# Seven block products for eight: a three-network MLP on one TensorE, with its weight operands kept in memory

## The chip, the cores and the metric

One core of a Trainium2 chip runs the whole program. The metric is the device time of one execution in microseconds (us), the median of three runs. Engines are named as in the profile: PE (matrix multiply), PEld (its weight load), DVE (vector), ACT (scalar), POOL (GpSimd) and SP (the queue that issues the DMAs).

## The reference, cut to what matters

The input x is 2 sequences of 2048 tokens with 512 features, in float32. Three two-layer networks (two shared, one chosen per sequence) with 2048 inner units run on every token. They are mixed with three gate weights per sequence, which depend on its first token, and a 512x512 layer chosen per sequence follows.

```
def _dense(x, wi_, wo_):
    return jax.nn.relu(x @ wi_) @ wo_
...
s0 = _dense(x, swi[0], swo[0]);  s1 = _dense(x, swi[1], swo[1])
h = jax.nn.relu(jnp.einsum('bsd,bdf->bsf', x, wi_sel))
eo = jnp.einsum('bsf,bfd->bsd', h, wo_sel)
gate_in = jnp.concatenate([eo[:, 0], s0[:, 0], s1[:, 0]], axis=-1)
w = jax.nn.softmax(jax.nn.relu(gate_in @ g1) @ g2, axis=-1)
x = x + eo * w[:, 0] + s0 * w[:, 1] + s1 * w[:, 2]
x = x + (x @ W[cat] + b[cat])
```

## The kernel before, in words

Precision comes from splitting. Each float32 operand becomes a high part, rounded to fp32r by ACT, and a low part, the rest, by DVE. `product` then does three matmuls for each one of the mathematics (high by high, low by high, high by low), 128x128 weights against 512 tokens each.

The 4096 tokens are taken in four *supers* of 1024, two blocks of 512. A super goes through 24 slices of 256 inner units, 8 for each network. For a slice SP loads the raw weights (`load_weights`), ACT makes the high parts (`split_high`) and DVE the low ones (`split_low`), so every super splits every weight again. PE runs *units*: `up` gives 128 inner units of one block in PSUM (`hps`), ACT and DVE turn them into `hh` and `hl` with the relu, `down` multiplies them into four PSUM banks (`yps`), and DVE adds these to `Y` in SBUF (`accumulate`). While PE runs one unit's `down`, the next unit's `up` is already done: the order is written out by hand in `steps`, and engines meet by semaphores only. Each engine takes its instructions in order, SP too.

Between supers the tokens of the next are transposed by PE (`transpose_x`). The sums are mixed by DVE (`mix`) in the first units of the next super, and the category layer (`category`, 48 full-width matmuls a block) runs after units 5 and 7 there, with `out_tiles` taking its result from PSUM. The gate of a sequence is computed once, at the end of its first super (`gate_partial`, `gate_hidden`, `gate_logits`). POOL clears buffers and rebuilds tokens (`xaux`, `gaux`) as high plus low.

Of the kernel before, what the change touches and what calls it, by code (L numbers as in the profile page):

```python
# [12 lines left out]
P = 128  # L31
D = 512
F = 2048
# [7 lines left out]
GC = GF // P  # L41
GROUPS = NETS * F // GF
PAIRS = GROUPS // 2
NET_PAIRS = PAIRS // NETS
WCOLS = KD * GF + GC * D
PIECE = 512
PIECES = WCOLS // PIECE
WARM_UP = 6
UNITS = 8
GATE_PART = [1, 2, 0]  # L50

def mixed(s):

    return NETS * KD * s

def mix_net(s):

    return 0 if s == SUPERS - 1 else 2  # L60

def build(nc, x, expert_id, category_id, wi, wo, swi, swo, g1, g2, W, bias, out):

# [9 lines left out]

    ctx = ExitStack()
    with ctx:
        def sb(name, shape, dt=F32):
            return ctx.enter_context(nc.sbuf_tensor(name, shape, dt))

        def sem(name):  # L80
            return ctx.enter_context(nc.semaphore(name))

        xh = sb("xh", [P, 2, 2, KD, TB], F32R)
        xl = sb("xl", [P, 2, 2, KD, TB], F32R)

        Y = sb("Y", [P, NETS, 2, KD, TB])
        wh = sb("wh", [P, 2, WCOLS], F32R)
        wl = sb("wl", [P, 2, WCOLS], F32R)  # L90
        wraw = sb("wraw", [P, 2, WCOLS])
        hh = sb("hh", [P, 2, TB], F32R)
        hl = sb("hl", [P, 2, TB], F32R)
        Wh = sb("Wh", [P, KD, D], F32R)
        Wl = sb("Wl", [P, KD, D], F32R)
        xaux = sb("xaux", [P, KD, TB])
        gaux = sb("gaux", [P, KD, D])
        gacc = sb("gacc", [P, D])
        bias_bc = sb("bias_bc", [P, D])
        ident = sb("ident", [P, P])  # L100
        ones = sb("ones", [P, P])
        g2s = sb("g2s", [P, KD, NETS])
        gt = sb("gt", [P, KD])
# [6 lines left out]
        ids = sb("ids", [1, 4], I32)  # L110

        yps = [ctx.enter_context(nc.psum_tensor(f"yps{j}", [P, TB], F32)) for j in range(KD)]
        hps = [ctx.enter_context(nc.psum_tensor(f"hps{j}", [P, TB], F32)) for j in range(2)]

        aps = [ctx.enter_context(nc.psum_tensor(f"aps{j}", [P, TB], F32)) for j in range(2)]

        s_ids = sem("ids_loaded")
        s_x = [sem("x_loaded_even"), sem("x_loaded_odd")]
        s_x0 = [sem("first_tokens_loaded_0"), sem("first_tokens_loaded_1")]
        s_w0 = [sem("first_up_weights_loaded_0"), sem("first_up_weights_loaded_1")]  # L120
        s_w0rdy = sem("first_up_weights_ready")
        s_w = [sem("weights_loaded_0"), sem("weights_loaded_1")]
        s_g = sem("gaux_loaded")
        s_g2 = sem("g2_loaded")
        s_bias = sem("bias_loaded")
        s_stored = [sem("out_stored_block_0"), sem("out_stored_block_1")]
        s_c = sem("ident_set")
        s_ident = sem("ident_cleared")
        s_ones = sem("ones_set")
        s_xtr = sem("x_transposed")  # L130
        s_xhi = sem("x_high_split")
        s_xlo = sem("x_low_split")
        s_whi = sem("weights_high_split")
        s_wrdy = sem("weights_ready")
        s_hps = sem("hidden_in_psum")
        s_hhi = sem("hidden_high_split")
        s_hrdy = sem("hidden_ready")
        s_yps = sem("net_out_in_psum")
        s_yacc = sem("net_out_accumulated")
        s_zero = sem("net_out_cleared")  # L140
        s_gused = sem("gaux_used")
        s_gch = sem("gate_vector_step")
        s_gps = sem("gate_product_in_psum")
        s_grelu = sem("gate_hidden_ready")
        s_gexp = sem("gate_exp_ready")
        s_gmix = sem("gate_product_ready")
        s_gmax = sem("gate_max_ready")
        s_xs = sem("x_summed")
        s_mix = [sem("mix_step_block_0"), sem("mix_step_block_1")]
        s_chi = sem("x2_high_split")  # L150
        s_clo = sem("x2_low_split")
        s_Wi = sem("category_identity_added")
        s_Whi = sem("category_high_split")
        s_Wrdy = sem("category_ready")
        s_ops = sem("out_in_psum")
        s_oev = sem("out_evacuated")

        block = ctx.enter_context(nc.Block())

        @block.sync
        def _(sp):
            def load_weights(s, net, p, j, e):

                m = s * GROUPS + net * 2 * NET_PAIRS + 2 * p + j
                f0 = p * 2 * GF + j * GF
                c0 = p * 2 * GC + j * GC
                if not isinstance(m, int) or m >= 2:
                    sp.wait_ge(s_wrdy, m - 1)
                src_i, src_o, n = (swi_v, swo_v, net) if net < 2 else (wi_v, wo_v, e)  # L170
                sp.dma_start(wraw[:, j, 0:KD * GF].rearrange("p (k f) -> p k f", k=KD),
                             src_i[n, :, :, bass.ds(f0, GF)]).then_inc(s_w[j], 16)
                sp.dma_start(wraw[:, j, KD * GF:WCOLS].rearrange("p (c d) -> p c d", c=GC),
                             src_o[n, :, bass.ds(c0, GC), :]).then_inc(s_w[j], 16)

            for h in range(2):
                ks = slice(2 * h, 2 * h + 2)
                sp.dma_start(xaux[:, :, 2 * h * P:(2 * h + 2) * P],  # L180
                             x_blk[0, :, :, 2 * h * P:(2 * h + 2) * P]).then_inc(s_x0[h], 16)
# [570 lines left out]
```

## Time and profile before

| | |
|---|---|
| median of 3 runs | 2220.74 us (2220.53 to 2221.44) |
| span of the profiled execution | 2218.0 us |
| PE busy | 2204.1 us (99%), 9772 instructions |
| DVE, ACT, POOL busy | 50%, 21%, 3% |
| DMA | 126.93 MB, mean 57 GB/s |
| PE clock | nine tenths or more of full speed in all 40 slices |

The table is to be read with care at one place: busy time of PE counts the modelled end of overlapping matmuls, so a matmul's mean duration is not its share of the time. Starts are what counts for PE. For DVE, ACT and POOL durations are real, and neighbours overlap by a little.

### The profile page before, as it was taken

How to read it: one execution, taken by the hardware profiler on the slowest of the kernel's cores; microseconds unless marked ns; L12 is line 12 of the kernel's file. 1: busy time of each engine (PE TensorE's matmuls, PEld its weight loads, DVE VectorE, ACT ScalarE, POOL GpSimd, SP SyncE). 2: the span in 40 equal slices, each digit the busy share in tenths (PEclk: the TensorE clock that was granted, in tenths of full speed). 3: DMA queues.
4: the chain of work that ended last, by engine and by line, in shares of the span. 5: the costliest groups of instructions: out<-in, count | busy, mean ns of one | idle time of the engine just before them, and what ended most of it. 6: DMA issues, size and time to landing. Idle time of an engine off the chain costs nothing.

```text
span 2218.0 us, 26621 instructions
## 1 busy us (share of the span) xinstructions
PE 2204.1 (99%) x9772; PEld 1825.4 (82%) x9772; DVE 1115.2 (50%) x1784; ACT 471.3 (21%) x847; POOL 65.8 (3%) x29
## 2 busy tenths in 40 slices
PE   9999999999999999999999999999999999999999
PEld 7888888887888888888888888888878888888887
DVE  4445454446744444444564455454466444444456
ACT  3212121222221212122212212121221221212121
POOL 1000000001000000000100000000010100000000
PEclk9999999999999999999999999999999999999999
DMA  3112121111111211111212121211111211111100
GB/s 133 62 57 87 46 76 57 57 38 57 57 57 57 67 46 57 38 57 38 76 38 100 38 95 38 76 62 51 57 57 38 76 38 57 38 57 43 52 19 39
DMA packets 85569, 126.93 MB, mean 57 GB/s; under 512 B 4116, under 2 KB 54292, under 8 KB 83732
## 3 DMA queue, kind: packets, MB, share of 16 engines
q1 hardware_dynamic: 85524, 126.37, 16.7%
q8 instruction: 23, 0.38, 0.1%
q14 instruction: 22, 0.18, 0.0%
HBM read 117.97 MB, written 8.39 MB: 57 GB/s over the span
## 4 chain that ended last, share of the span: by engine, by line
PE 99%; issue 0%; DMA 0%; DVE 0%; SPq 0%; ACT 0%; DVEq 0%
PE hps L602 47%; PE yps L602 47%; PE aps L602 4%; PE aps L642 1%; DMA xaux<-in_x_dram 0%; DVE gp L434 0%; PE aps L659 0%; ACT hh L295 0%; DVE hl L374 0%; DVE Y L491 0%; SPq L180 0%; SPq L182 0%; DVEq L395 0%
## 5 line engine op out<-in xcount | busy, mean ns | idle before, releaser
L374 DVE SCALAR_TENSOR_TENSOR hl<-hps,hh 128x512 fp32r<-128x512 f32 x384 | 265.1, 690 | 1033.9 <-ACT hh L295 1031.8
L602 PE MATMUL hps<-xh,wh 128*128 128x512 f32 x1536 | 600.4, 391 | 0.0
L602 PE MATMUL hps<-xh,wl 128*128 128x512 f32 x1536 | 599.2, 390 | 0.0
L602 PE MATMUL hps<-xl,wh 128*128 128x512 f32 x1536 | 599.1, 390 | 0.0
L602 PE MATMUL yps<-hh,wh 128*128 128x512 f32 x1536 | 598.3, 390 | 0.0
L602 PE MATMUL yps<-hh,wl 128*128 128x512 f32 x1536 | 597.7, 389 | 0.0
L602 PE MATMUL yps<-hl,wh 128*128 128x512 f32 x1536 | 597.5, 389 | 0.0
L295 ACT ACTIVATE hh<-hps 128x512 fp32r<-128x512 f32 x384 | 229.6, 598 | 1676.9 <-PE hps L602 1676.9
L396 DVE TENSOR_TENSOR Y<-yps,Y 128x512 f32<-128x512 f32 x728 | 450.0, 680 | 0.0
L602 PEld LDWEIGHTS hps<-xh,wl 128*128 128x128 f32 x1536 | 289.2, 188 | 60.3
L602 PEld LDWEIGHTS hps<-xh,wh 128*128 128x128 f32 x1536 | 289.1, 188 | 60.0 <-DVE wl L557 0.4
L602 PEld LDWEIGHTS hps<-xl,wh 128*128 128x128 f32 x1536 | 289.3, 188 | 59.7
L602 PEld LDWEIGHTS yps<-hh,wh 128*128 128x128 f32 x1536 | 288.6, 188 | 59.9
L602 PEld LDWEIGHTS yps<-hh,wl 128*128 128x128 f32 x1536 | 288.2, 188 | 60.1
L602 PEld LDWEIGHTS yps<-hl,wh 128*128 128x128 f32 x1536 | 288.5, 188 | 59.7
L382 DVE TENSOR_TENSOR wl<-wraw,wh 128x512 fp32r<-128x512 f32 x382 | 238.4, 685 | 0.0
L302 ACT ACTIVATE wh<-wraw 128x512 fp32r<-128x512 f32 x382 | 208.6, 623 | 0.0
L280 POOL TENSOR_TENSOR xaux<-xh,xl 128x2048 f32<-128x2048 f32 x4 | 18.4, 4612 | 1448.0 <-issue 919.7
L602 PE MATMUL aps<-Wl,xh 128*128 128x512 f32 x128 | 49.8, 389 | 0.0
L602 PE MATMUL aps<-Wh,xh 128*128 128x512 f32 x128 | 49.8, 389 | 0.0
L602 PE MATMUL aps<-Wh,xl 128*128 128x512 f32 x128 | 49.8, 389 | 0.0
L491 DVE TENSOR_TENSOR Y<-aps,bias_bc 128x512 f32<-128x512 f32 x32 | 22.0, 689 | 47.8 <-PE aps L602 47.8
(52 smaller groups left out, 382.5 us busy)
## 6 DMA issues: line engine op xcount, KB each, us to landing
wraw<-in_L_cond_swi_dram SPq DMA_DIRECT2D x63, 512.0 KB, 3.4
wraw<-in_L_cond_swo_dram SPq DMA_DIRECT2D x63, 512.0 KB, 4.7
wraw<-in_L_cond_wi_dram SPq DMA_DIRECT2D x32, 512.0 KB, 3.4
wraw<-in_L_cond_wo_dram SPq DMA_DIRECT2D x32, 512.0 KB, 4.8
out_dram<-Y SPq DMA_DIRECT2D x7, 1024.0 KB, 4.0
gaux<-in_L_cond_g_dram SPq DMA_DIRECT2D x6, 1024.0 KB, 8.1
xaux<-in_x_dram SPq DMA_DIRECT2D x6, 1024.0 KB, 6.0
gaux<-in_L_cond_W_dram SPq DMA_DIRECT2D x2, 1024.0 KB, 7.9
```

The costliest lines, as they stand in the source:

```text
L280: pool.tensor_tensor(into[:, :, :], xh[:, q, k, :, :].bitcast(F32), xl[:, q, k, :, :].bitcast(F32), ALU.add).then_inc(s_xs, 1)
L295: act.activation(hh[:, i % 2, :], hps[i % 2][:, :], ACT.Relu).then_inc(s_hhi, 1)
L302: act.activation(wh[:, slot, cols], wraw[:, slot, cols], ACT.Copy).then_inc(s_whi, 1)
L374: dve.scalar_tensor_tensor(out=hl[:, i % 2, :], in0=hps[i % 2][:, :], scalar=0.0, in1=hh[:, i % 2, :].bitcast(F32), op0=ALU.max, op1=ALU.s ...
L382: last = dve.tensor_tensor(wl[:, slot, cols], wraw[:, slot, cols], wh[:, slot, cols].bitcast(F32), ALU.subtract)
L396: dve.tensor_tensor(Y[:, net, k, d, :], yps[d][:, :], Y[:, net, k, d, :], ALU.add).then_inc(s_yacc, 1)
L491: dve.tensor_tensor(Y[:, 1, k, t, :], aps[T % 2][:, :], bias_bc[:, :], ALU.add).then_inc(s_oev, 1)
L602: last = pe.matmul(dst, stationary[a], moving[b], start=start and i == 0, stop=stop and i == 2)
L642: last = pe.transpose(aps[X % 2][:, t * P:(t + 1) * P], src[:, t, d * P:(d + 1) * P], ident[:, :])
```

## The change

The product of a token matrix and a weight matrix is cut into 2x2 blocks: tokens by block of 512 (two) and features by half (two), weights likewise. Seven products of sums of blocks replace the eight (Strassen's scheme in Winograd's form). One *step* is now a slice of 256 inner units of one network for all 1024 tokens; there are 96. In a step PE runs seven `up` products and seven `down` products, each of six full-width matmuls, alternating: `up(n, i)` of the next step, then `down(d, i)` of this one. I call the time of one such alternation a *period*.

What the seven products need in addition:

- Sums of token blocks (`XT`), once a super, by POOL (`token_sum`).
- Sums of weight blocks, by POOL (`up_sums`, `down_sums`, four subtractions or additions each). They are split and, in the 24 steps of super 0 and the 8 of the other sequence's own network (super 2, network 2), written by SP to memory (`keep_up`, `keep_down`). These 32 steps are called *prepared*. In the other 64 the split sums are read back, product by product (`load_up`, `load_down`), and nothing is split.
- Sums of hidden blocks: DVE combines the seven up results (`block_step`, five a step), ACT applies the relu, POOL subtracts (`hidden_sums`), ACT and DVE split.
- Seven accumulators `ACC` of 1024 elements. DVE adds each product's pair of PSUM banks (`add_sum`), ACT copies in a network's first step of an even super (`begin_sum`). Where a network ends the sums go to memory (`spill`) and come back as `MB` or `MR` for mixing in the next super, a quarter at a time, with `mix_scale` (DVE) and `mix_add` (POOL).

Down products, tokens' transposes, gate and category results all go through a ring of two PSUM pairs `rps`: `next_pair` waits until the entry two before was taken. The category layer now has 12 parts of 24 matmuls in supers 1 to 3, each behind `up(n, 4)`, and four at the end.

```
-                for d in range(KD):
-                    if c == 0 and not (isinstance(K, int) and K == 0):
-                        pe.wait_ge(s_yacc, KD * K + d + 1 - KD)
-                    c0 = KD * GF + c * D + d * P
-                    last = product(yps[d][:, :], (wh[:, slot, c0:c0 + P], wl[:, slot, c0:c0 + P]),
-                                   (hh[:, v % 2, :], hl[:, v % 2, :]), c == 0, c == GC - 1)
+            def next_pair(kind, i):
+                e = turn[0]
...
+                turn[0] += 1
+                if e >= 2:
+                    pe.wait_ge(*taken(e - 2))
+                return rps[e % 2]
+            def up(n, i):
...
+                for q in range(2):
+                    cols = slice(q * P, (q + 1) * P)
+                    toks = slice(q * TB, (q + 1) * TB)
+                    ins = product(ups[UP_BANK[i]][:, :], (WU[:, i, 0, cols], WU[:, i, 1, cols]),
+                                  (XH[:, i, toks], XL[:, i, toks]), q == 0 and i < 4, q == 1)
+            def down(n, i):
+                dst = next_pair("sum", PRODUCTS * n + i)
...
+                for j in range(2):
+                    cols = slice(j * P, (j + 1) * P)
+                    ins = product(dst[:, j, :], (WD[:, i, 0, cols], WD[:, i, 1, cols]),
+                                  (HH[:, i, :], HL[:, i, :]), True, True)
+            def category(s, c):
+                dst = next_pair("out", 4 * s + c)
+                pe.wait_ge(s_ml, 4 * s + c + 1)
...
+            for m in range(-1, STEPS):
+                n, d = m + 1, m
+                for i in range(PRODUCTS):
+                    if n < STEPS:
+                        up(n, i)
+                    for kind, k in ring_extra(m, i):
...
+                    if d >= 0:
+                        down(d, i)
```
The sums by POOL, and the way of the raw down blocks: SP may load new ones only when the low parts of the last are made.
```
+            def hidden_sums(n):
...
+                pool.tensor_tensor(HT[:, 2:4, :], hid[:, 1:3, :], hid[:, 0:2, :], ALU.subtract).then_inc(s_T, 1)
...
+                pool.tensor_tensor(HT[:, 4, :], hid[:, 2, :], HT[:, 2, :], ALU.subtract).then_inc(s_T, 1)
...
+                pool.tensor_tensor(HT[:, 6, :], HT[:, 5, :], HT[:, 4, :], ALU.subtract).then_inc(s_T, 1)
+            def blocks_down(n, experts):
+                if PREP[n] >= 1:
+                    sp.wait_ge(s_wld, 2 * PREP[n])
...
+                for slot, a, c in ((0, 0, 0), (7, 1, 0), (6, 1, 1), (5, 0, 1)):
+                    sp.dma_start(PD[:, slot, :], src[e, :, c0 + c, a * HB:(a + 1) * HB]).then_inc(s_pd, 16)
+            def down_high(n, late):
...
+                act.wait_ge(s_Sd, 4 * PREP[n] + (4 if late else 3))
+                act.activation(WD[:, part, 0, :], PD[:, part, :], ACT.Copy).then_inc(s_whd, 1)
+            def down_low(n, late):
...
+                dve.tensor_tensor(WD[:, part, 1, :], PD[:, part, :], WD[:, part, 0, :].bitcast(F32),
+                                  ALU.subtract).then_inc(s_wld, 1)
```

Two places show how the queues stand. The first is DVE in a weight-splitting stretch. Before, it has four splits of 512 (`wl`) between two hidden low parts (`hl`), and four adds (L396) after every second of these, here in the first slices:
```order
L374 SCALAR_TENSOR_TENSOR hl<-hps,hh 128x512
L382 TENSOR_TENSOR wl<-wraw,wh 128x512 x4
L374 SCALAR_TENSOR_TENSOR hl<-hps,hh 128x512
L396 TENSOR_TENSOR Y<-yps,Y 128x512 x4
L374 SCALAR_TENSOR_TENSOR hl<-hps,hh 128x512 x2
```
Now, in a whole prepared period, it has these (`WU`, `WD` are low parts of weights, `HL` of hidden blocks, `ACC` the adds, the three rows at L951 `block_step`):
```order
L887 TENSOR_TENSOR WU<-PU,WU 128x4x256
L903 TENSOR_TENSOR HL<-HT,HH 128x1024
L923 TENSOR_TENSOR ACC<-rps,ACC 128x1024
L893 TENSOR_TENSOR WD<-PD,WD 128x4x256
L906 TENSOR_TENSOR HL<-HT,HH 128x1536
L923 TENSOR_TENSOR ACC<-rps,ACC 128x1024 x2
L887 TENSOR_TENSOR WU<-PU,WU 128x3x256
L951 TENSOR_TENSOR u_59<-ups,p_58 128x512
L951 TENSOR_TENSOR u_60<-ups,u_59 128x512
L951 TENSOR_TENSOR hid<-ups,u_60 128x512
L923 TENSOR_TENSOR ACC<-rps,ACC 128x1024
L893 TENSOR_TENSOR WD<-PD,WD 128x3x256
```
Behind these come an add, the low part of `hid`, and two block steps with an add behind each. Splits now stand between the adds on which PE's ring waits, and read buffers that POOL has written.

The second place is a period with a part of the category layer, on DVE. Its result leaves PSUM at L1030 now:
```order
L926 SCALAR_TENSOR_TENSOR ACC<-rps,gw,ACC 128x1024 [waits sum_added,down_product]
L1022 TENSOR_TENSOR MXL<-MX,MXH 128x1024 [waits mix_high]
L926 SCALAR_TENSOR_TENSOR ACC<-rps,gw,ACC 128x1024 [waits sum_added,down_product]
L899 TENSOR_TENSOR HL<-hid,HH 128x1024 [waits hidden_high_parts]
L951 TENSOR_TENSOR hid<-ups,u_59 128x512 [waits up_product]
L1030 TENSOR_TENSOR OUT<-rps,bias_bc 128x1024 [waits bias_loaded,out_in_psum]
```
On PE, in the same period, the 24 category matmuls (their last is the first row here) stand ahead of `down(d, 4)`:
```order
L1179 MATMUL rps<-WcH,MXL 128x512
L1179 MATMUL rps<-HH,WD 128x512 [waits down_operand_loaded_4,hidden_low_parts,sum_added]
L1179 MATMUL rps<-HL,WD 128x512
L1179 MATMUL rps<-HH,WD 128x512 x2
L1179 MATMUL rps<-HL,WD 128x512
L1179 MATMUL rps<-HH,WD 128x512
L1179 MATMUL ups<-XH,WU 128x512 [waits up_operand_loaded_5,hidden_block_step]
L1179 MATMUL ups<-XL,WU 128x512
L1179 MATMUL ups<-XH,WU 128x512 x2
L1179 MATMUL ups<-XL,WU 128x512
L1179 MATMUL ups<-XH,WU 128x512
L1179 MATMUL rps<-HH,WD 128x512 [waits down_operand_loaded_5,hidden_low_parts,out_evacuated]
```
Before, these matmuls had two PSUM buffers (`aps`) of their own; now they hold a pair of the ring of the down products, and `down(d, 5)` waits for its release.

## Rows read from the trace of the kernel before

**Rows 1.** The page: busy time, granted clock, the chain that ended last
```profile
PE 2204.1 (99%) x9772; PEld 1825.4 (82%) x9772; DVE 1115.2 (50%) x1784; ACT 471.3 (21%) x847; POOL 65.8 (3%) x29
PEclk9999999999999999999999999999999999999999
PE 99%; issue 0%; DMA 0%; DVE 0%; SPq 0%; ACT 0%; DVEq 0%
```
**Rows 2.** Timeline (start, duration), PE: first and last of 96 category matmuls
```profile
2192.36 0.39 PE L602 MATMUL aps<-Wh,xh 128*128 128x512 f32 x1
...
2213.90 0.39 PE L602 MATMUL aps<-Wh,xl 128*128 128x512 f32 x1
```
**Rows 3.** Timeline, start of the program: first up matmul, eight transposes, first down
```profile
10.41 0.77 PE L602 MATMUL hps<-xh,wh 128*128 128x512 f32 x1
...
17.90 1.04 PE L642 MATMUL aps<-ident,gaux 128*128 128x128 f32 x8
...
18.69 0.47 PE L602 MATMUL yps<-hh,wh 128*128 128x512 f32 x1
```
**Rows 4.** Timeline, PE around the first gate; idle time before in brackets
```profile
546.25 1.05 PE L659 MATMUL aps<-gp,ones 128*128 128x3 f32 x8 [3.16 <-DVE gp L434]
...
548.30 0.63 PE L602 MATMUL hps<-xl,wh 128*128 128x512 f32 x1
548.73 0.63 PE L602 MATMUL hps<-xh,wl 128*128 128x512 f32 x1
...
551.29 0.47 PE L602 MATMUL hps<-xh,wl 128*128 128x512 f32 x1
```
**Rows 5.** Timeline, end of the program, DVE's last instruction
```profile
2214.32 0.69 DVE L491 TENSOR_TENSOR Y<-aps,bias_bc 128x512 f32<-128x512 f32 x1 [2.03 <-PE aps L602]
```
**Rows 6.** Timeline, DVE and ACT: four instructions back to back
```profile
546.11 2.47 DVE L396 TENSOR_TENSOR Y<-yps,Y 128x512 f32<-128x512 f32 x4
553.03 2.49 DVE L382 TENSOR_TENSOR wl<-wraw,wh 128x512 fp32r<-128x512 f32 x4
19.55 2.20 ACT L302 ACTIVATE wh<-wraw 128x512 fp32r<-128x512 f32 x4
```
**Rows 7.** The page's costliest groups: ACT, busy us, mean ns, idle before
```profile
L295 ACT ACTIVATE hh<-hps 128x512 fp32r<-128x512 f32 x384 | 229.6, 598 | 1676.9 <-PE hps L602 1676.9
```
**Rows 8.** Timeline, POOL: memsets of 4096 and 2048, additions of 2048
```profile
5.00 3.51 POOL L269 MEMSET Y<- 128x4096 f32 x1
...
541.38 4.54 POOL L280 TENSOR_TENSOR gaux<-xh,xl 128x2048 f32<-128x2048 f32 x1
...
1732.44 1.81 POOL L288 MEMSET Y<- 128x2048 f32 x1 [27.56 <-DMA out_dram<-Y]
...
1738.78 4.62 POOL L280 TENSOR_TENSOR gaux<-xh,xl 128x2048 f32<-128x2048 f32 x1
```
**Rows 9.** Timeline, DVE while POOL adds
```profile
536.89 1.29 DVE L403 TENSOR_TENSOR xl<-aps,xh 128x512 fp32r<-128x512 f32 x2 [1.15 <-ACT xh L308]
540.70 5.50 DVE L434 TENSOR_SCALAR gp<-g2s,gt 128x3 f32<-128x3 f32 x4
1742.28 3.47 DVE L382 TENSOR_TENSOR wl<-wraw,wh 128x512 fp32r<-128x512 f32 x4
```
**Rows 10.** DMA: issue of one on SP; by line, KB and median us to landing; queue's bytes and share
```profile
305.87 0.37 SPq L171 DMA_DIRECT2D wraw<-in_L_cond_wi_dram  x1
...
wraw<-in_L_cond_swi_dram SPq DMA_DIRECT2D x63, 512.0 KB, 3.4
out_dram<-Y SPq DMA_DIRECT2D x7, 1024.0 KB, 4.0
gaux<-in_L_cond_g_dram SPq DMA_DIRECT2D x6, 1024.0 KB, 8.1
out_dram<-Y SPq DMA_DIRECT2D x4, 256.0 KB, 2.5
q1 hardware_dynamic: 85524, 126.37, 16.7%
```

More of the change, by code:

```diff
@@ new lines, in net_of, with slice_of, prepared, weight_set @@
+def net_of(n):
+    return n % STEPS_SUPER // STEPS_NET
+def slice_of(n):
+    return n % STEPS_NET
+def prepared(n):
+    return n < STEPS and (super_of(n) == 0 or (super_of(n) == 2 and net_of(n) == 2))
+def weight_set(n):
+    return net_of(n) * STEPS_NET + slice_of(n) + (STEPS_NET if net_of(n) == 2 and super_of(n) >= 2 else 0)
+PREP = [sum(prepared(i) for i in range(n)) for n in range(STEPS + 1)]
+SETS = (NETS + 1) * STEPS_NET
+def copied(n):
+    return slice_of(n) == 0 and (super_of(n) % 2 == 0 or net_of(n) == 0)
@@ new lines, in build, with taken @@
+        s_tail = sem("tail_pool_step")
+        s_tadd = sem("tail_vector_step")
+        plan = ring_plan()
+        place_in_ring = {entry: e for e, entry in enumerate(plan)}
+        def taken(e):
+            kind, i = plan[e]
+            if kind == "tokens":
+                return s_xs, i + 1
+            if kind == "gate":
+                b = sum(1 for o in plan[:e] if o == (kind, i))
+                return (s_grelu, b + 1) if i == 0 else (s_gexp, b + 1)
+            if kind == "out":
+                return s_oev, i + 1
+            n = i // PRODUCTS
+            if copied(n):
+                return s_acp, PRODUCTS * COPIES[n] + i % PRODUCTS + 1
+            return s_acc, i + 1 - PRODUCTS * COPIES[n]
@@ L349, in _, with staged @@
[L349 to L367 removed]
+            def staged(k, h):
+                return XS[:, k, h, :, :].rearrange("p j t -> p (j t)")
@@ L728, in _ @@
-            for k in range(2):
-                category(SUPERS - 1, k)
+                pe.matmul(ups[3][:, 0:P], ones[:, :], ones[:, :], start=True, stop=True)
+            for i in range(4):
+                transpose_tokens(i)
+            for m in range(-1, STEPS):
+                n, d = m + 1, m
+                for i in range(PRODUCTS):
+                    if n < STEPS:
+                        up(n, i)
+                    for kind, k in ring_extra(m, i):
+                        if kind == "tokens":
+                            transpose_tokens(k)
+                        elif kind == "out":
+                            category(k // 4, k % 4)
+                        elif k == 0:
+                            gate_hidden(m // (2 * STEPS_SUPER))
+                        else:
+                            gate_logits(m // (2 * STEPS_SUPER))
+                    if d >= 0:
+                        down(d, i)
```

1502 lines of the change are left out of this document (969 added, 533 removed).

## The prediction

> **What bounds the kernel now.** I read the page first, for the busiest engine and the last chain: PE is busy 99% of the span and the chain that ended last lies on it for 99% [rows 1]. The reader is to see that nothing else is near: DVE 50%, POOL 3%. So the time is PE's matmuls, and I need their spacing, not their duration. The timeline gives it: 96 category matmuls start from 2192.36 to 2213.90, 95 gaps, so 0.2267 us each [rows 2]. A full-width product of six takes U = 1.36 us. 9600 matmuls (9216 of the networks, 384 of the category layer) make 2176 of 2218 us. Then I looked at the ends [rows 3, 5], at the one place where PE stands, the gate [rows 4], and at what DVE, ACT, POOL and the DMAs cost apiece [rows 6 to 10], since the change loads these.
>
> **What it removes.** Each step has 7 x 12 = 84 matmuls for 96: 96 x 84 + 384 = 8448, 1152 fewer. At 0.2267 that is -261.2 us. The profiled execution would go from 2218.0 to 1956.8. A period of 14 products is 19.05 us if PE never waits. All else below is added.
>
> **DVE's price list.** Four adds of 512 take 2.47 us and one 0.69 [rows 6, 5]: 0.60 apiece back to back, of which 0.53 is 512 elements and 0.06 fixed. So 1024 costs 1.13, 1536 1.66, 768 0.86. The low parts of weights go alike (2.49 for four). A plain period has seven adds (7.9), five block steps (3.0, and 0.3 as three wait for one another) and low parts of 1024, 1024, 1536 (3.9): 15.1 us under 19.05. ACT does four of 512 in 2.20 and one in 0.60 [rows 6, 7], so I take 1.04 for 1024; it has about 6 us. POOL: memsets of 4096 and 2048 differ by 1.70 us, leaving 0.11 fixed [rows 8]; an addition of 2048 at 4.6 gives 2.36 for 1024, 1.24 for 512, 0.67 for 256. I walked a plain period in queue order with these: the `up` product 3 ends at 9.7, `hid` is split at 16.1, POOL's sums end at 22.3, and they are first needed at 24.5 and later; the closest add is 1 us early. Plain periods stay PE's, at nothing.
>
> **Prepared periods (30).** DVE has 4.0 more for low parts of weights: 19.1, level with PE, so each stall now shows. They come from the port. POOL's addition ran 1738.78 to 1743.40; the four DVE splits that started at 1742.28 took 3.47 for 2.49, one second more, about until POOL ended [rows 8, 9, 6]. Four tiny `gp` steps at 540.70 took 5.50, to the end of POOL's addition of 541.38 [rows 8, 9]. But DVE's 536.89, one input in PSUM, took its 1.29 beside a running addition [rows 9]. The Trainium skill's page "SBUF — State Buffer" (Who interferes with whom) says that a DVE instruction with two SBUF inputs and a GpSimd one that reads SBUF shut each other out for a whole instruction. The trace agrees, as above; it speaks against this change, which puts 11 POOL sums beside 7 such DVE instructions in a prepared period.
> Worked through: after block step 3, DVE needs 4.0 to reach `HL` 2:4, but relu 0.6, the 1024 sum 2.4, the weight split that holds the port 1.2, and the 512 sum 1.2 end at 5.5. Stall 1.45. Then `down_low` meets the third sum (0.1), `HL` 4:7 waits for ACT (0.4), three splits meet weight sums (0.7). That makes 21.75. Next, the down blocks' round trip: from `down_low`'s end, SP issues one store and four loads (0.37 and a wait each, 2.2), the last lands 2.0 after (stores of 256 and 1024 KB land in 2.5 and 4.0, so 2.0 is fixed) and queues behind the 1 MB store (some 1.3): 5.5 [rows 10]. Three sums 2.1, ACT 0.8: 8.4, against 8.7 of DVE's own work in between. With jitter I take 22.0, so +2.95 in 26 periods; +1.5 in the four where ACT copies instead of DVE's adding: 82.7. Lowest 0 (DVE keeps PE's pace); highest by the row that landed in 8.1 us [rows 10], 2.6 later: 24.3, +60 more. Without the port's part (0.8 of the small meetings) the sum would be 24 less.
>
> **Category parts (12), +58.** PE is ready after `up(n, 4)` at 12.25. `MXL` stands behind block steps 0 to 2 (start 9.75, end 11.86) and an add: 12.9 to 14.1. PE waits 1.9. 24 matmuls (5.44) and `down(d, 4)` end at 20.95. DVE then adds, splits `hid`, does a block step, and only then empties the category pair: 21.1 + 1.13 + 1.13 + 0.6 + 1.2 = 25.2, while PE reached `down(d, 5)` at 22.3. PE waits 2.9. 4.84 x 12 = 58.1; nothing hides it, since PE's own queue is the cover. 
>
> **Start, +17.** Before, the first `down` starts at 18.69 [rows 3]; 24 up matmuls (5.4) and 32 transposes (eight take 1.04) are work, so 9.2 is lead. Now all raw tokens (2 MB), four copies, four POOL sums of 2.36 in a chain, seven high and low parts and the second weight step precede `down(0, 0)`: transposes to 15, token sums 16.6 to 26.2, low parts to 31.5, weights of step 1 and block steps to 36.3, the last two `up` products to 39.5. Less 9.5 for 42 matmuls and 4.1 of transposes 25.9, so 16.7 more.
>
> **Between supers, +23.** Five token low parts (5.65) fall in one period, two (2.3) in the next, POOL sums three tokens beside them (port, 2): +9.1 behind each prepared stretch (two), +4.5 at the plain one.
>
> **End, +12.** Now the last matmul's slot ends 3.9 us before the span does [rows 2]. After: the last period runs 2.2 late on `HL`, then an add, four tail adds and 2048-wide splits leave PE idle for 7.2, 1.6 of slow clock follow, and the last part of 1024 with its 512 KB store takes 4.8. 15.8 less 3.9.
>
> **Small ones, +28.** `gate_partial` and `category_low` in prepared periods 8, spills ahead of `down` blocks 5, `mix_scale` (1.9) and POOL's mixing beside low parts in 24 periods 8, scaling and token transposes in the ring 8; the gates cost what they cost now (-1). `load_up`/`load_down` at nothing: 3.7 MB a period is 193 GB/s, each load has 17 us, and the queue's 126.37 MB in 16.7% of the span means 341 GB/s [rows 10].
>
> **Sum.** 1956.8 + 82.7 + 58.1 + 8 + 16.7 + 22.7 + 11.9 + 28 = 2184.9. The median stands 2.7 above the span (2220.7 against 2218.0): **2188 us**. Of 261 us saved some 228 are handed back.
>
> **Rivals.**
> - *POOL and DVE keep out of each other's way and prepared periods run at PE's 19.05.* DVE's 19.1 of work speaks for it, the 3.47 row against it. 2188 - 83 = 2105. With category waits also partly hidden, 2085.
> - *The down blocks come late* (the other side). In each prepared period they must land before `down_low(n, 0)`. At 8.1 us, as for `gaux`, the period is 24.3: 2188 + 26 x 2.3 = 2248. It decides from 33 us lost, 1.3 a period, a landing of 7.0 us. For it: loads of `gaux` at 8.1 were behind others, as these are. Against: 512 KB alone took 3.4.
> - *It comes out even*: my terms a seventh too small, 2216 to 2225.
> That the change does not do what it says is excluded: the program has 8448 such matmuls.
>
> **Chances.** Forecast (2145 to 2215) 0.48; prepared at PE's pace (2085 to 2145) 0.22; even 0.05; late blocks and the like (over 2225) 0.25. A measurement here tells 0.2%, 4.4 us. Range: from 2105, the first rival's time, to 2248, the second's; each leaves out about 1 in 10. Faster 0.69, same 0.05, slower 0.26.
>
> **What would show it.** Periods of 19.1 in steps 25 to 47 away from category parts and about 22 in 1 to 22; DVE near 85% there, `HL` waiting for POOL; idle of 1.9 and 2.9 on PE ahead of and behind each category part, on `MXL` and `OUT`; the first down product at 39 us; 8 us idle before the last 96 matmuls. I am wrong if prepared periods are below 20 or above 24, if plain ones exceed 20 (loads late, POOL's instructions dearer than 0.11 fixed), or if category parts cost nothing.

## The result, and the profile after

The changed kernel takes 2393.5 us, the kernel before, on the same chips, 2220.6. The ratio is 1.078 (95% interval 1.076 to 1.081): slower by 7.8%, where I forecast 2188 (faster by 1.5%) and a range up to 2248. The time lies outside the range and on the other side of no change. The four runs of the changed kernel lie from 2388.2 to 2402.8, wider than the 4.4 us that I had taken for a measurement here; where an experiment below has one run, I read nothing into a few us.

The page of the kernel after, which answers to [rows 1]: busy times, the granted clock in 40 slices, and the chain that ended last, by engine.
```profile
PE 2098.8 (88%) x8620; PEld 1656.9 (69%) x8620; DVE 1861.0 (78%) x1667; ACT 858.5 (36%) x1033; POOL 903.2 (38%) x663
PEclk8999999999899999999999999999989999999998
...
PE 19%; DVE 7%; issue 5%; DMA 4%; POOL 3%; SPq 1%; ACT 1%; DVEq 0%; ACTq 0%; POOLq 0%
```
PE has its 1152 instructions fewer, as the sum had it. But it fell from 99% to 88% busy. The last chain lay on it for 99% before. Now the chain could be followed back only to 1417 us, so that its shares add to 40% of the span, and PE holds 19, under half of it. No single wait took its place: DVE, DMA, POOL and SP all have a part. So I cut the program at ACT's copy of `up` product 0, which stands once in each period, and read the stretches one by one:

| stretch | measured us | forecast us | missed |
|---|---|---|---|
| start, and the first period | 25.1 + 22.0 | about 41 | 6 |
| prepared, super 0: 23 periods | 587.5 | 517 | 70 |
| mixing, super 1: 16 periods | 402.2 | 364 | 38 |
| rest of super 1: 8 periods | 169.5 | 157 | 12 |
| super 2 up to its prepared part: 16 periods | 356.8 | 353 | 4 |
| prepared, super 2: 8 periods | 220.8 | 187 | 34 |
| mixing, super 3: 16 periods | 400.2 | 364 | 36 |
| plain periods at the end of super 3 | 19.0 each | 19.05 | 0 |
| from the last of them to the end | 73.4 | 64 | 9 |

The forecast column shares out the terms of the prediction: 23 prepared periods at 22.0 with three of them shorter by 1.5, the transition's 9.1 and some 6 of the small ones make 517, and so on. The column on the right adds to 209 for 205.5 missed, since the shares are rounded and the two periods in which PE transposes tokens ahead of super 2 (some 4 us, part of the 1956.8) are not shared out. Half of it (104) lies in the prepared stretches and another third (74) in the mixing ones. Neither part is of one kind. In super 0, seventeen ordinary periods took 24.2 on average, 37 us more than 22.0 each; the four around a change of network (25.8 and 28.9, 25.8 and 27.7) were 23 over, the one in which the category matrix is split (29.3) 7, and the transition (39.0) 8. Of the 74, some 27 lie in the eight periods with a category part (33.3 on average, in the shares 30.0) and some 47 in the others.

**A prepared period.** DVE's timeline over one whole period of super 0 (start, duration, idle time before in brackets):
```profile
142.23 2.23 DVE L887 TENSOR_TENSOR WU<-PU,WU 128x1024 fp32r<-128x1024 f32 x1 [0.52 <-ACT WU L685]
144.38 2.31 DVE L903 TENSOR_TENSOR HL<-HT,HH 128x1024 fp32r<-128x1024 f32 x1
146.62 1.21 DVE L923 TENSOR_TENSOR ACC<-rps,ACC 128x1024 f32<-128x1024 f32 x1
147.75 1.21 DVE L893 TENSOR_TENSOR WD<-PD,WD 128x1024 fp32r<-128x1024 f32 x1
148.88 2.28 DVE L906 TENSOR_TENSOR HL<-HT,HH 128x1536 fp32r<-128x1536 f32 x1
...
158.75 0.96 DVE L893 TENSOR_TENSOR WD<-PD,WD 128x768 fp32r<-128x768 f32 x1 [1.14 <-ACT WD L694]
...
166.12 2.23 DVE L887 TENSOR_TENSOR WU<-PU,WU 128x1024 fp32r<-128x1024 f32 x1 [0.52 <-ACT WU L685]
```
POOL beside it:
```profile
142.09 1.29 POOL L574 TENSOR_TENSOR HT<-hid,HT 128x512 f32<-128x512 f32 x1
143.46 2.15 POOL L579 TENSOR_TENSOR HT<-HT 128x512 f32<-128x512 f32 x1
148.41 1.14 POOL L528 TENSOR_TENSOR PU<-PU 128x256 f32<-128x256 f32 x1 [2.80 <-DMA PU<-in_L_cond_swi_dram]
149.51 2.25 POOL L529 TENSOR_TENSOR PU<-PU 128x256 f32<-128x256 f32 x1
...
155.38 0.74 POOL L538 TENSOR_TENSOR PD<-PD 128x256 f32<-128x256 f32 x1 [2.10 <-DMA PD<-in_L_cond_swo_dram]
```
SP and ACT on the way of the down blocks:
```profile
148.98 0.34 SPq L359 DMA_DIRECT2D wd_kept<-WD  x1
149.37 3.21 SPq L348 DMA_DIRECT2D PD<-in_L_cond_swo_dram  x4
...
157.87 0.85 ACT L694 ACTIVATE WD<-PD 128x768 fp32r<-128x768 f32 x1 [5.16 <-POOL PD L542]
```
The reader is to see two things. First, the rows of 1024 at 142.23 and 144.38 take 2.23 and 2.31 where the same shape takes 1.21 at 147.75, and POOL's 512 sum at 143.46 takes 2.15 where the one before it took 1.29. The two engines leapfrog: DVE's `WU` waits for POOL's sum to end at 143.38, POOL's next one then waits behind it, and DVE's `HL` behind that one. With 0.5 on L906 (1.75 where nothing is in its way) this is 2.7 us. These rows bear out the Trainium skill's rule on the port ("SBUF — State Buffer", Who interferes with whom), by which a DVE instruction with two SBUF inputs and a GpSimd one that reads SBUF do not run together. Second, from the end of `down_low` (148.88) over the store, the four issues, the landing (155.38), three sums and ACT it takes 9.8 us to 158.72, and DVE waits for 1.14 of it.

**A mixing period with its category part.** PE, then DVE, in super 1, around its two waits:
```profile
781.97 0.77 PE L1179 MATMUL rps<-WcH,MXH 128*128 128x512 f32 x1 [3.78 <-issue]
782.53 0.63 PE L1179 MATMUL rps<-WcL,MXH 128*128 128x512 f32 x1
782.96 0.63 PE L1179 MATMUL rps<-WcH,MXL 128*128 128x512 f32 x1
...
795.84 0.50 PE L1179 MATMUL rps<-HH,WD 128*128 128x512 f32 x1 [2.88 <-DVE OUT L1030]
```
```profile
768.71 2.35 DVE L903 TENSOR_TENSOR HL<-HT,HH 128x1024 fp32r<-128x1024 f32 x1 [1.65 <-POOL HT L574]
...
775.03 1.14 DVE L1014 TENSOR_SCALAR MR<-MB,gw 128x1792 f32<-128x1792 f32 x1
...
780.65 1.22 DVE L1022 TENSOR_TENSOR MXL<-MX,MXH 128x1024 fp32r<-128x1024 f32 x1
```
and the two waits of such a part in super 2:
```profile
1335.65 0.47 PE L1179 MATMUL rps<-WcH,MXH 128*128 128x512 f32 x1 [1.95 <-issue]
...
1348.52 0.50 PE L1179 MATMUL rps<-HH,WD 128*128 128x512 f32 x1 [2.82 <-DVE OUT L1030]
```
In super 2 they are 1.95 and 2.82, where I had 1.9 and 2.9. In supers 1 and 3 the first is 3.78, since the scaling of the next sums (1.14) and an `HL` that waited 1.65 and then took 2.35 for 1.21 stand ahead of `MXL` on DVE. Over the twelve parts the two waits add to 37.4 and 33.4 us, 70.8 for the 58 of the sum. In the mixing periods without a category part PE stands behind DVE too; DVE's scaling waits for its sums, by the costliest groups:
```profile
L1017 DVE SCALAR_TENSOR_TENSOR MR<-MB,gw,MR 128x1792 f32<-128x1792 f32 x16 | 33.4, 2085 | 32.2 <-DMA MB<-sums_kept 32.2
```

**Start, transition, tail.** POOL's queue where super 0 ends, and the last wait of PE:
```profile
609.14 0.73 POOL L538 TENSOR_TENSOR PD<-PD 128x256 f32<-128x256 f32 x1 [10.92 <-DMA PD<-in_L_cond_wo_dram]
...
612.11 4.65 POOL L564 TENSOR_TENSOR XT<-XS 128x1024 f32<-128x1024 f32 x2
```
```profile
2340.79 12.02 POOL L651 TENSOR_TENSOR XS<-XS,ACC 128x1024 f32<-128x1024 f32 x4 [2.35 <-DVE ACC L926]
...
2361.97 0.77 PE L1179 MATMUL rps<-WcH,XH 128*128 128x512 f32 x1 [12.12 <-DVE XL L1158]
```
The token sums that the next super waits for stand behind down sums that wait 10.9 us for their load; that period is 39.0 us long. The transition behind super 1 has no down sums and took 29.4 for the 23.6 of the sum: there POOL's token sums run beside DVE's low parts of tokens and hidden blocks (3.38 and 2.17 for 1.22 at 1183.53 and 1188.02, 2.76 for 1.75 at 1180.84), and PE stands 3.53. At the start, POOL's first sum for step 1 waits until 31.87 for raw weights whose loads are issued from 27.88, behind DVE's low part of the last ones, and the first `down` comes some 5 us later than the 39.5 forecast. Before the last 96 matmuls PE stands 12.1 us, where I had 7.2.

### The profile page after: what moved, and what is told of

Its sections match the earlier page's. It is cut to its first block and busy times, and to the rows that moved or that the text cites. A ratio compares the mean times of both kernels' runs of the same rounds, so it can differ in the third digit from the quotient of the medians.

```text
span 2391.1 us, 26920 instructions
## 1 busy us (share of the span) xinstructions
PE 2098.8 (88%) x8620; PEld 1656.9 (69%) x8620; DVE 1861.0 (78%) x1667; ACT 858.5 (36%) x1033; POOL 903.2 (38%) x663
## 5 line engine op out<-in xcount | busy, mean ns | idle before, releaser
L1179 PE MATMUL rps<-HH,WD 128*128 128x512 f32 x2688 | 984.1, 407 | 194.1 <-DVE ACC L923 103.4
L1179 PE MATMUL ups<-XH,WU 128*128 128x512 f32 x2688 | 972.6, 403 | 40.9 <-DVE hid L951 18.6
L1179 PEld LDWEIGHTS rps<-HH,WD 128*128 128x128 f32 x2688 | 518.0, 193 | 372.0 <-DVE ACC L923 143.0
L1179 PEld LDWEIGHTS ups<-XH,WU 128*128 128x128 f32 x2688 | 524.2, 195 | 172.5 <-DVE hid L951 32.1
L1179 PE MATMUL ups<-XL,WU 128*128 128x512 f32 x1344 | 539.0, 401 | 0.0
L1179 PE MATMUL rps<-HL,WD 128*128 128x512 f32 x1344 | 536.2, 399 | 0.0
L926 DVE SCALAR_TENSOR_TENSOR ACC<-rps,gw,ACC 128x1024 f32<-128x1024 f32 x322 | 408.1, 1277 | 128.0 <-PE rps L1179 127.7
L923 DVE TENSOR_TENSOR ACC<-rps,ACC 128x1024 f32<-128x1024 f32 x294 | 355.0, 1215 | 63.9 <-PE rps L1179 63.5
L1179 PEld LDWEIGHTS ups<-XL,WU 128*128 128x128 f32 x1344 | 262.9, 196 | 55.2
L1179 PEld LDWEIGHTS rps<-HL,WD 128*128 128x128 f32 x1344 | 259.7, 193 | 48.2
L906 DVE TENSOR_TENSOR HL<-HT,HH 128x1536 fp32r<-128x1536 f32 x96 | 181.3, 1888 | 6.3 <-ACT HH L733 6.3
L951 DVE TENSOR_TENSOR hid<-ups,u 128x512 f32<-128x512 f32 x192 | 132.1, 688 | 17.1 <-PE ups L1179 8.0
L899 DVE TENSOR_TENSOR HL<-hid,HH 128x1024 fp32r<-128x1024 f32 x96 | 119.6, 1246 | 15.3 <-ACT HH L726 14.1
L887 DVE TENSOR_TENSOR WU<-PU,WU 128x768 fp32r<-128x768 f32 x64 | 101.9, 1592 | 36.6 <-ACT WU L685 36.5
```

Source lines behind the costliest of these rows:

```text
L887: dve.tensor_tensor(WU[:, part, 1, :], PU[:, part, :], WU[:, part, 0, :].bitcast(F32), ALU.subtract).then_inc(s_wlu, 1)
L899: dve.tensor_tensor(HL[:, 0:2, :], hid[:, 0:3:2, :], HH[:, 0:2, :].bitcast(F32), ALU.subtract).then_inc(s_hlo, 1)
L906: dve.tensor_tensor(HL[:, 4:7, :], HT[:, 4:7, :], HH[:, 4:7, :].bitcast(F32), ALU.subtract).then_inc(s_hlo, 1)
L923: dve.tensor_tensor(ACC[:, i, :, :], src[:, :, :], ACC[:, i, :, :], ALU.add).then_inc(s_acc, 1)
L926: dve.scalar_tensor_tensor(out=ACC[:, i, :, :], in0=src[:, :, :], scalar=gw[:, g:g + 1], in1=ACC[:, i, :, :], op0=ALU.mult, op1=ALU.add).t ...
L951: dve.tensor_tensor(dst, ups[bank][:, :], other, ALU.add).then_inc(s_ev, 1)
```

## The experiments

### Waits, one at a time

**The mixing orders.** ACT's `mix_high` goes right behind `hidden_high(d, 2)`, and on DVE `mix_low` and `finish_out` go ahead, to these places:
```
                 if d >= 0:
                     add_sum(d, 1)
+                for ms, c, stage in mixing:
+                    if stage == MIX_PERIODS:
+                        mix_low(ms, c)
...
+                for ms, c, stage in mixing:
+                    if stage == MIX_PERIODS:
+                        finish_out(ms, c)
                 if d >= 0:
                     add_sum(d, 4)
```

> Only the order of three instructions changes in the 12 periods with a category part: MXH and MXL are made early in the period, and the category pair is emptied ahead of the add of down product 4. Theory Q (DVE's queue order makes PE stand there): the idle of 3.8 us ahead of each category part, the 2.9 us for OUT and the slow clock behind them (2.4 us) go; such periods fall from 33.4 to about 26 in supers 1 and 3 and from 30.5 to about 25 in super 2, in all -85 us: 2308. Rival L (DVE's whole load in such a period bounds it, whatever the order): about 31 a period, -20 us: 2373.

Measured: 2301.0. The 33.4 us of a period with a category part (29.5 to 33.8 in super 2) became 24.6, about its 84 and 24 matmuls (24.5). The twelve are 98 us shorter together, the other periods some 6 longer.

**No preparation.** One set of prepared weights for all 96 steps (`prepared(n)` is `n == 0`).

> Leaves out the weight preparation of all steps but the first: every step reads the split weight sums of step 0 back from memory, so the output is that of another network. Theory W (what the 32 prepared steps cost is their own DVE, POOL and SP work): all periods of super 0 and of network 2 in super 2 fall from 24 to 29 down to 19.0, about -195 us: 2198. Rival C (the loss is of the scheme as such, by slow clock and port, in all steps): such periods stay at 21 or more, -130 us or less: 2260 or more.

Measured: 2217.2. The ordinary periods of super 0 fall to 19.0. So preparation cost 176 us, where my term was 83 and a share of the small ones; and without any of it the kernel is still only even with the kernel before.

**POOL reads nothing.** Each POOL sum of hidden and weight blocks becomes memsets of nearly its duration (2.3 us for 2.4, 1.15 for 1.29, 0.57 for 0.74).
```
-                pool.tensor_tensor(HT[:, 2:4, :], hid[:, 1:3, :], hid[:, 0:2, :], ALU.subtract).then_inc(s_T, 1)
+                filled(HT[:, 2:4, :], 4).then_inc(s_T, 1)
```

> Leaves out the sums of hidden blocks and of weight blocks: POOL fills the same places with a constant, in the same time (2.4, 1.3 and 0.7 us), at the same places in its queue, but reads no SBUF. Theory P (the port that DVE's second SBUF input shares with POOL's reads lengthens prepared periods): HL of 1024 and WU of 1024 fall from 2.3 and 2.2 to 1.2 us, prepared periods from 23.9 to about 21.7, in all -66 us: 2327. Rival R (the round trip of the down blocks bounds the period): HL and WU fall, but the wait of WD grows by as much and the period stays within 0.5 of 23.9: 2380 or more.

Measured: 2341.7. By the costliest groups (busy, mean ns, idle before), first of the kernel after, then of this one:
```profile
L903 DVE TENSOR_TENSOR HL<-HT,HH 128x1024 fp32r<-128x1024 f32 x96 | 197.3, 2055 | 65.1 <-POOL HT L574 58.3 <-ACT HH L729 6.8
...
L887 DVE TENSOR_TENSOR WU<-PU,WU 128x1024 fp32r<-128x1024 f32 x32 | 67.1, 2096 | 24.4 <-ACT WU L685 24.4
...
L893 DVE TENSOR_TENSOR WD<-PD,WD 128x768 fp32r<-128x768 f32 x32 | 30.6, 957 | 50.7 <-ACT WD L694 50.7
```
```profile
L915 DVE TENSOR_TENSOR HL<-HT,HH 128x1024 fp32r<-128x1024 f32 x96 | 117.3, 1222 | 52.0 <-POOL HT L535 45.2 <-ACT HH L741 6.8
...
L899 DVE TENSOR_TENSOR WU<-PU,WU 128x1024 fp32r<-128x1024 f32 x32 | 40.6, 1267 | 26.2 <-ACT WU L697 26.2
...
L905 DVE TENSOR_TENSOR WD<-PD,WD 128x768 fp32r<-128x768 f32 x32 | 31.1, 971 | 85.9 <-ACT WD L706 85.9
```
The stretched instructions go back to 1.22 and 1.27 us: 107 us of DVE's time in these two groups is the port's. Only 52 reach the end, since the wait for the down blocks grows by 35. Even of the 52 not all need be the port's: the memsets are 0.1 to 0.2 us shorter than the sums (the three of the down blocks' trip 1.8 us for 2.4), and no run takes that apart.

**Blocks ahead of the store**, in one place of SP's order:
```
-                        if prepared(d):
-                            keep_down(d, 1)
                         if prepared(n) and n > 0:
                             blocks_down(n, experts)
+                        if prepared(d):
+                            keep_down(d, 1)
```

> SP issues the four loads of the next down blocks ahead of the 1 MB store instead of behind it. Theory R (the round trip behind the store is part of the period): the first sum of down blocks starts some 3 us earlier, DVE's wait for WD (1.14 us a prepared period, 5.4 where a network begins) goes, prepared periods fall from 23.9 to 22.8, and those that begin a network from 29 to 25: -40 us, 2353. Rival P (the port alone bounds it): nothing but a fraction of a microsecond, 2385 to 2395.

Measured: 2353.4. The four loads are issued in 1.80 us instead of 3.21:
```profile
143.64 1.80 SPq L348 DMA_DIRECT2D PD<-in_L_cond_swo_dram  x4
145.48 0.43 SPq L359 DMA_DIRECT2D wd_kept<-WD  x1
```
**Both of these.**

> Both of the last two edits together, so it too leaves out the sums of hidden and weight blocks. Alone they took 49 and 37 us. Theory B (port and round trip lie in one loop of DVE's, each hiding part of the other; what they add together is most of the gap to 19.05): with POOL reading nothing the wait for WD had grown to 2.7 to 4 us, and blocks first removes it: prepared periods of about 20.5, -110 us: 2281, more than the sum of the two. Rival S (they are separate terms): -86 us, 2305, periods of 21.7.

Measured: 2278.1. Alone they gave 52 and 40, together 115: each had hidden part of the other. Prepared periods are near 20.4, the memsets' share included.

**The slow clock.** Matmuls without use (8 in super 2, 16 in supers 1 and 3) are put into the category's pair, ahead of the wait for `MXL`.

> PE runs 16 extra full-width matmuls (8 in super 2) into the category pair while it waits for MXL; the category part then overwrites them, so the result is unchanged. Theory K (the slow clock behind the wait costs what the rows show, 12 matmuls at 0.43 for 0.23 us): the category matmuls all run 0.227 apart, periods with a part in supers 1 and 3 fall from 33.4 to 31, -23 us in all: 2370. Rival N (the clock falls because of both waits and the tail of DVE's work behind them sets the period anyway): within 8 us of 2393.

Measured: 2395.3. The category matmuls now start 0.227 apart, where twelve stood 0.427 apart in the kernel after. The two mixing stretches took 402.1 and 397.5 us for 402.2 and 400.2: the 23 us of theory K do not come. Their periods with a category part did get 11 us shorter in all, and the ones between them longer by about 8. That DVE's loop over several periods sets their sum, and the clock does not, fits this but is argued. (Super 0, which the edit does not touch, took 5 us more, so one run cannot tell a gain of a few us from none.)

### Orders that do nothing, or harm

**`hid` split ahead of add 4**, and the fourth block step as well:
```
                 if n < STEPS:
                     hidden_low(n, 0)
                     block_step(n, 3)
+                if d >= 0:
+                    add_sum(d, 4)
```

> Only DVE's order changes: the add of down product 4 goes behind the low part of hid and block step 3, so POOL's sums start 1.2 us earlier against DVE's next need of them. Theory H (DVE arrives at HL 2:4 before POOL's second sum is done, and this stall is part of each DVE-bound period): the stall of 0.5 to 1.65 shrinks, -1.0 us in the 30 prepared periods and the 24 with mixing: -45 us, 2348. Rival R (PE's ring needs that add, and a new wait of PE takes its place): 0 or slower, plain periods of over 19.05: 2393 to 2420.

Measured: 2455.6, slower by 62. DVE now stands for ACT's high parts and for PE, by its waits (us, times, longest):
```profile
DVE hid L951 <- PE ups L1179: 108.2, 12, 10.2
DVE HL L899 <- ACT HH L726: 106.6, 80, 2.8
```
In the kernel after, the two were 8.0 and 14.1. Neither was in my account of the chain: the add had filled the time that ACT needs for the relu and the high part. In the mixing periods DVE then comes to a block step whose `up` product PE has not reached. How the 62 us divide between the two was not worked out.

**The orders so far, with two token sums ahead of the down sums**, this one included:

> The mix order, the blocks first and the hid order together, and POOL sums two of the next super's tokens ahead of the down blocks instead of behind them. Theory (the terms add up: -92, -37, -40, and 7 us at each of two supers' ends): 2393 - 183 = 2210. Rival (they hide one another, and DVE's own 19.1 us with POOL's port in prepared periods holds the rest): 2240.

Measured: 2254.1. Transitions fell from 39.0 and 36.5 to 30.2 and 29.5.

**Low part behind the add** (`hidden_low(d, 1)` and `add_sum(d, 0)` exchanged), alone:

> The kernel after with one exchange on DVE: in each period the add of down product 0 goes ahead of the low parts of hidden sums 2 and 3 (1024 elements). In the trace of after that low-part instruction runs 2.3 us for 1.2 in prepared periods, since POOL's subtraction into HT or a weight sum holds the port when it starts. Theory P (the place behind POOL's sum costs it): started an add later (1.15 us) it meets no POOL instruction and takes 1.2, the ring gets its add earlier, and 1.1 us go in the 30 prepared and some 24 mixing periods: about 2340. Rival T (another wait takes its place: the period is set by the trip of the down blocks from DVE's low parts over SP, DMA, POOL and ACT back to DVE, which an exchange inside it shortens only by what it brings forward): the wait of L893 for ACT's high parts grows by what the low part gives back, 2385 to 2400. What decides between them in the trace is the duration of L903's 1024-element group and the idle time ahead of L893.

Measured: 2393.2, no difference. The duration goes and the wait comes:
```profile
L903 DVE TENSOR_TENSOR HL<-HT,HH 128x1024 fp32r<-128x1024 f32 x96 | 131.2, 1366 | 2.2 <-POOL HT L574 2.2
...
L893 DVE TENSOR_TENSOR WD<-PD,WD 128x768 fp32r<-128x768 f32 x32 | 30.6, 957 | 85.8 <-ACT WD L694 85.8
```
66 us of port time and 63 of waiting for POOL left that group. The wait for the down blocks grew from 50.7 to 85.8, and DVE's wait for PE ahead of the adds at L926 from 127.7 to 186.5. That is theory T for the prepared periods. The mixing ones have no such trip, and there another wait took the place; that this was the wait for the sums' loads is likely by the run with the early loads further down, but no run shows it for this kernel.

### Orders together

**All orders but the harmful one:** the mixing orders, blocks ahead of the store, two token sums ahead of the down sums, and the low part behind the add.

> Orders only, the work unchanged: the mixing orders of the first experiment (2393 to 2301, -92), the down blocks issued ahead of the stores of the last split parts (-40), two of the next super's token sums ahead of the down sums where a super ends (some -15 by the run that had them together with others), and the add ahead of the low part (as in the run beside this one). If all add up and theory P holds for the last: 2393 - 92 - 40 - 15 - 50 = 2196, below the kernel before. If theory T holds: 2238 to 2250, above it. Prepared periods would be near 21.5 in the first case and 22.7 in the second.

Measured: 2222.9, between the two; that is even with the kernel before.

**And tail and category split**: the tail's four sums by DVE, the category matrix split in steps that are not prepared.
```
-                if m == 13:
+                if m == STEPS_SUPER + 2:
                     category_identity(0)
```

> The run beside this with two more orders: the four sums of the tail by DVE instead of POOL (POOL took 12.0 us for them in the trace of after, DVE takes 1.2 apiece: about -6 where PE stood idle 12.1), and the category matrix split in the first steps of supers 1 and 3, which are not prepared (POOL's sums of it took 2.5, 1.9 and 2.8 us in prepared periods of 29.3 us: some -8). Together 14 less than the run beside this: 2182 by theory P, about 2225 by theory T, the second even with the kernel before within 1%.

Measured: 2214.6, ratio to the kernel before 0.9969 (0.9953 to 0.9986). That is 8 less than the run before for the 14 expected.

**The exchange undone**, from there:

> The last run's kernel with its add of down product 0 put back behind the low parts of hidden sums 2 and 3, nothing else. That exchange alone moved the kernel after by 0 (2393.2 for 2393.5), though the low part went from 2055 to 1366 ns. Theory T' (it was hidden behind the trip of the down blocks; once these are issued ahead of the stores the trip no longer ends last, and the exchange counts): this kernel is slower than the last run (2214.6) by 0.9 us in 26 prepared periods, 2235 to 2240, with prepared periods of 22.7 for 21.8. Rival (it counts nowhere, and the sum of the orders was larger for another reason): 2212 to 2217.

Measured: 2242.0, ratio 1.0087 (1.0070 to 1.0104), prepared periods 22.7 for 21.8. The exchange that did nothing alone is worth 27 us once the down blocks' trip is short. Theory T' held.

**Sums loaded earlier**, from the 2214.6 kernel. SP's order:
```
-                            if ms % 2 == 0 and i == 0 and stage in (1, 2):
-                                mix_sums(ms, c, stage)
+                            if ms % 2 == 0 and i == 5 and stage in (0, 1):
+                                mix_sums(ms, c, stage + 1)
+                            if ms % 2 == 0 and i == 5 and stage == 2 and c < 3:
+                                mix_sums(ms, c + 1, 0)
...
```

> The last run's kernel with one move on SP: the loads of network sums for mixing are issued a third of a period earlier, behind the load of down operand 5 of the period before, as soon as the scaling before has read the buffer. In the last run the load was issued at 805.73, the scaling waited for it until 813.39 (2.98 idle), and PE stood 2.12 and 0.52 behind the adds that queue behind the scaling. Theory M (mixing periods of supers 1 and 3 are set by this load): 2.6 us go in the 16 periods with a scaling and no category part, less in the 8 with one: about -42, 2172. Rival (DVE's own loop of 17.2 us of work and the low part's waits set them): within 8 of 2214.6.

Measured: **2179.6**, ratio 0.9817 (0.9800 to 0.9833). A scaling by the timeline, in the 2214.6 kernel and in this one:
```profile
813.39 2.08 DVE L1012 SCALAR_TENSOR_TENSOR MR<-MB,gw,MR 128x1792 f32<-128x1792 f32 x1 [2.98 <-DMA MB<-sums_kept]
```
```profile
693.93 2.07 DVE L1015 SCALAR_TENSOR_TENSOR MR<-MB,gw,MR 128x1792 f32<-128x1792 f32 x1
```
The wait is gone. Behind the first category part, mixing periods without one are 20.0 to 21.0 us for 22.1 to 24.6, and those with one 24.0 for 24.0 to 24.8; the two mixing stretches are 34 us shorter together. Both kernels are beaten, with the work of the change as it was: the orders differ, and four tail sums have moved from POOL to DVE. That 2179.6 is near the forecast's 2188 does not bear out its sum: the waits for `MXL` and `OUT` at the category parts, 58 us of it, are gone here, with 0.3 us ahead of six parts left.

**The weights' low part behind the add too.**

> The run beside this with one exchange more on DVE: in prepared periods the low parts of the weight sums 3 to 6 (1024 elements) go behind the add of down product 0. They run 2.2 us for 1.15 in the last run, from 270.19, waiting for POOL's addition that ends at 271.34, and POOL's next one then runs 2.16 for 1.3 behind them. If the place decides: 1.0 in 30 prepared periods, 30 less than the run beside this, about 2142. If the low part meets POOL's next sum instead (it starts at the same 271.3), or the trip of the down blocks ends last again: within 5 of the run beside this.

Measured: 2197.5, ratio 0.9890 (0.9873 to 0.9906): slower by 18 than the run beside it, where 30 less or within 5 had been expected: both theories fall. Two rows of DVE in a prepared period:
```profile
274.63 1.22 DVE L885 TENSOR_TENSOR WU<-PU,WU 128x1024 fp32r<-128x1024 f32 x1
275.76 2.31 DVE L901 TENSOR_TENSOR HL<-HT,HH 128x1024 fp32r<-128x1024 f32 x1
```
`WU` takes 1.22 now, and the next instruction meets POOL's last hidden sum instead. The collision has moved by one instruction, and periods that begin or end a network came out longer (25.5 for 23.2 in super 2, say). Why these lose what the others don't was not followed further.

## Why the prediction was wrong, step by step

**Bound and removal: right.** The 1152 matmuls are gone and the plain periods run at 19.0 for 19.05. What failed is the sum of what is handed back: 228 us forecast, 434 measured (the span of 2391.1 less 1956.8).

**"Prepared periods (30)": the step that failed first, by most of 104 us.** (Some 13 of the 104 are the two transitions in these stretches.) The mechanism was named and both its parts exist, but each was too small. The port: I walked one collision at full price and several "small meetings" (1.45 + 0.1 + 0.4 + 0.7); the rows show 2.7 us on three instructions and 0.5 for ACT. I had not seen that an instruction of POOL delayed by DVE delays DVE's next, so that one meeting becomes three. The 24 us for which the prediction has the port's part are too few by its own walk, too: they count the small meetings and leave out the 1.2 that POOL waits for the weight split inside the 1.45. The down blocks' trip: 8.4 us "against 8.7 of DVE's own work", measured 9.8. Of the 1.4 more, 1.5 is SP's issue (3.7 us from the end of `down_low`, for 2.2), 0.4 the sums and ACT, and the landing took 0.5 less than I had. My walk had a margin of 0.3 and came to 22.0; it was 23.9. Since the two parts overlap, a sum of them was the wrong form: without POOL's reads 52, with the shorter trip 40, with both 115. Periods around a change of network were a second thing missed: there SP's four issues take up to 5.70 us (at 246.28, in the period of 28.9, which became 25.7 with the blocks first), and I had the ones in which ACT copies 1.5 shorter than the others, not longer. With the orders mended the ordinary periods run at 21.8, close to the forecast's 22.0, which had been the time of a better-ordered kernel.

**"Category parts (12)": right in super 2, too small in supers 1 and 3.** `OUT` was 2.8 to 2.9 as forecast, but for one of 1.92. `MXL` was 1.95 to 2.01 for three parts of super 2 and 3.78 to 4.09 for three each in supers 1 and 3, where DVE does `mix_scale` for the next part in that very period and comes to it late; the last part of each super took 2.7 to 3.1. I had put `mix_scale` among "small ones" as DVE time and not into the queue ahead of `MXL`. The slow clock is in the trace (0.427 between twelve matmuls, 2.4 us a part). Filling the wait took it away from there and the total did not fall; whether the 8 us that I charged for it are in the 2393 stays open, since they are no more than runs differ by.

**"Small ones": mixing periods, some 47 of the 74 us missed (the rest is in the category parts).** I put 8 us on 24 periods for the scaling and POOL's mixing, and nothing on the load of its sums: "`load_up`/`load_down` at nothing" covered the weights only. The load was issued behind its turn on SP, landed after DVE had come to it, and stood in DVE's queue ahead of the adds on which PE's ring waits. Moving it, and nothing else, won 35 us, measured in the mended kernel and not in the kernel after.

**Start, transitions, tail.** The start was 6 too small, by raw weights of step 1 that land at 31.9. The transitions behind the prepared stretches were 8 and 5 too small: token sums stand in POOL's queue behind down sums that wait 10.9 us. The plain one was 6 too small (the other 6 of its row's 12 are the periods with transposes): by the rows, the port cost more than the 2 us that I put. The tail was 9 too small: its sums take 3.0 apiece at POOL, where DVE adds in 1.2.

**The rivals.** "The down blocks come late" was right in its mechanism: issued ahead of the store, the blocks gave back 40 us alone. It did not decide the sign by itself; with these 40 the kernel was still at 2353, and the mixing orders (92) and the sums' loads (35) were needed as well. Its price, 2.3 a period, was near what came on top of 22.0 in an ordinary period (1.9, the port's part included), which is luck, as part of that is not the blocks' (with them issued first 23.9 became 22.7). It gave 2248 alone, and the mixing periods are missing in it. The condition that I gave for it, a landing of 7.0 us, was not reached (6.5 from the end of `down_low`); it began to cost earlier, since the issues took longer and the sums and ACT too. That POOL and DVE keep out of each other's way is refuted. My chance for all of over 2225 was 0.25, too small for a case with four engines level and a margin of 0.3 us.

**Open:** what the remaining 2.7 us of a prepared period (21.8 for 19.05) consist of once the trip is short. DVE is busy for 254 of 280 us in such a stretch (100 to 380 us); one port meeting on `WU` is left by its row, and the try to remove it failed. Open as well is why that try, and the `hid` order before it, cost time.

## What to carry to other kernels

When a change takes work from the bounding engine and levels three or four others with it, the saved time is an upper bound, and what comes back is set by queue orders: walk each in-order queue, DMA issues included, through one whole period of each kind, and distrust any slack under a microsecond. Waits that overlap can be neither added up nor judged one at a time: an exchange that won nothing here was worth 27 us after another wait had gone. And a change that loses may be a good one badly ordered: the same work, put in another order in four queues and with four tail sums moved to another engine, went from 7.8% slower to 1.8% faster.

## What the runs showed of the hardware that I had not expected

- The four loads of the down blocks took SP mostly 1.8 to 2.0 us to issue where the last store was 2.5 us back (the run with the blocks first), 2.9 to 3.9 right behind the issue of one store, and 3.8 to 5.7 right behind two (5.70 at 246.28, in a period of 28.9 us). The issue time of a DMA is not a constant of 0.37.
```profile
245.30 0.47 SPq L353 DMA_DIRECT2D wu_kept<-WU  x1
245.81 0.43 SPq L359 DMA_DIRECT2D wd_kept<-WD  x1
246.28 5.70 SPq L348 DMA_DIRECT2D PD<-in_L_cond_swo_dram  x4
```
- Two engines that shut each other out from the port can do so in turns: POOL's 512 sum 2.15 for 1.29 and DVE's 1024 low part 2.31 for 1.21, one behind the other, and 5 us later POOL's 256 sum 2.25 for 0.74 behind DVE's 1536 low part, with no idle time that a list of waits would show. It is seen only in durations that differ between rows of one shape.
